# Routed blocks written out with constant waits, three engines' orders rearranged, a third up chunk in single-pass products

## What is computed

```python
def _ssm_forward(hidden_states, z, ...):            # z = layernorm(x)
    x = einsum('ed,bld->bel', in_proj_w, hidden_states)
    u = silu(conv4(x) + conv_b)
    dt_lo, Bm, Cm = split(einsum('ke,bel->bkl', x_proj_w, u))
    delta = softplus(einsum('er,brl->bel', dt_proj_w, dt_lo) + dt_proj_b)
    state = state * exp(d_t * A) + (d_t * u_t) * B_t          # scan over 512 steps, 16 states
    y = (state . C + D * u) * silu(z)

def _L0_ffn_ref(x, ...):                             # x = layernorm(x)
    aff = sigmoid(x @ wa); topk_p, topk_i = top_k(aff, 2); combine = normalised weights
    expert(x) = (gelu(x @ g + gb) * (x @ w1 + b1)) @ w2 + b2
    return x + sum of 2 shared experts + sum over 16 routed experts of combine * expert(x)
x = x + ssm;  x = x + ffn(layernorm(x))
```

## Time and profile before

| | us |
|---|---|
| median of 3 runs | 877.4 (876.62 to 882.0) |
| the profiled execution | 879.89 |
| its span | 877.7 |
| TensorE busy in the span | 784.8 |
| VectorE, ScalarE, GpSimd busy | 669.4, 524.3, 553.9 |

### The profile page before, as it was taken

The page is one execution under the profiler, slowest core; times in us unless marked ns, Lnnn a source line. Parts: engine busy times, 40 slices in busy tenths (PEclk is TensorE's granted clock), DMA queues, the critical chain, the costliest instruction groups (busy, mean ns, idle before and its releaser), DMA issues.

```text
span 877.7 us, 16086 instructions
## 1 busy us (share of the span) xinstructions
PE 784.8 (89%) x4384; PEld 587.4 (67%) x4385; DVE 669.4 (76%) x860; ACT 524.3 (60%) x884; POOL 553.9 (63%) x348
## 2 busy tenths in 40 slices
PE   6963799999999988998899999999999999999992
PEld 3622688888888877887777878886555555555550
DVE  4999999999999998999596759545656656565561
ACT  3896899999999999995332532023444333443330
POOL 9551399989999999999815560221434744454432
PEclk9975799999999999999999999999999999999996
DMA  6010311111141113201220121255558877876663
GB/s 183 1 55 0 106 52 62 56 54 51 59 157 49 49 49 109 60 14 49 97 96 1 49 90 55 96 228 238 115 142 242 215 208 186 186 196 177 159 139 48
DMA packets 35384, 91.65 MB, mean 104 GB/s; under 512 B 8716, under 2 KB 9228, under 8 KB 32000
## 3 DMA queue, kind: packets, MB, share of 16 engines
q1 hardware_dynamic: 23360, 65.50, 21.8%
q0 software_dynamic: 11968, 25.44, 14.3%
HBM read 122.24 MB, written 21.36 MB: 164 GB/s over the span
## 4 chain that ended last, share of the span: by engine, by line
PE 41%; DVE 17%; SPq 14%; issue 9%; POOL 8%; ACT 6%; DMA 3%; DVEq 0%; ACTq 0%; POOLq 0%
DVE r L1051 12%; PE ps L1451 6%; PE ps L1554 5%; PE ps L1453 5%; PE ps L1452 5%; POOL r L527 5%; PE ps L1577 5%; SPq L390 4%; SPq L391 3%; SPq L392 3%; PE ps L1790 3%; PE ps L1555 3%; SPq L393 3%; PE ps L1809 2%; POOL split L532 2%
## 5 line engine op out<-in xcount | busy, mean ns | idle before, releaser
L527 POOL TENSOR_TENSOR r<-r,mem 128x1024 f32<-128x1024 f32 x127 | 297.8, 2378 | 34.7 <-DVE r L1051 34.1
L1051 DVE TENSOR_TENSOR_SCAN r<-r,ps 128x1024 f32<-128x1024 f32 x128 | 286.8, 2277 | 9.7 <-issue 9.0
L752 ACT ACTIVATE r<-mem,nega 128x511 f32<-128x511 f32 x256 | 167.0, 715 | 1.8 <-DVE r L1051 1.7
L1554 PE MATMUL ps<-ident,mem 128*128 128x128 f32 x768 | 130.4, 279 | 28.4 <-DVE r L1051 21.7
L1577 PE MATMUL ps<-ident,r 128*128 128x128 f32 x1024 | 132.5, 273 | 3.7 <-DVE r L1081 2.4
L767 ACT ACTIVATE mem<-mem,b_turned 128x512 f32<-128x512 f32 x192 | 124.8, 715 | 8.6 <-PE ps L1555 8.0
L1554 PEld LDWEIGHTS ps<-ident,mem 128*128 128x128 f32 x768 | 87.4, 142 | 53.8 <-issue 52.8
L1577 PEld LDWEIGHTS ps<-ident,r 128*128 128x128 f32 x1024 | 115.8, 141 | 4.3 <-DVE r L1081 2.6
L1555 PE MATMUL ps<-mem 128*128 128x128 f32 x512 | 99.7, 277 | 0.0
L917 ACT COPY mem<-ps 128x256 f32<-128x256 f32 x47 | 17.5, 373 | 128.4 <-PE ps L1798 125.8
L1451 PE MATMUL ps<-split 128*128 128x512 f32 x216 | 87.3, 404 | 4.3 <-issue 1.7
(11 more groups left out here) (209 smaller groups left out, 1263.7 us busy)
## 6 DMA issues: line engine op xcount, KB each, us to landing
r<-in_r_up SPq DMA_DIRECT2D x47, 1024.0 KB
mem<-in_r_down SPq DMA_DIRECT2D x47, 512.0 KB
mem<-cm_rows SPq DMA_DIRECT2D x64, 256.0 KB, 3.2
mem<-in_r_b SPq DMA_DIRECT2D x4, 2048.0 KB, 12.3
out<-acc POOLq DMA_DIRECT2D x17, 256.0 KB, 2.9
r<-in_x SPq DMA_DIRECT2D x4, 1024.0 KB, 4.9
xn_scratch<-r SPq DMA_DIRECT2D x16, 256.0 KB, 2.7
mem<-in_ctx_t SPq DMA_DIRECT2D x4, 512.0 KB, 7.3
```

What stands on the lines that cost most here:

```text
L527: pool.tensor_tensor(state[:, k % 2, ec:ec + 2], state[:, k % 2, ec:ec + 2], c, ALU.mult).then_inc(s["weighed"], 1)
L752: act.activation(decay[:, k % 2, ec, 1:L], delta[:, b, ec, 1:L], ACT.Exp, scale=nega[:, ec, n:n + 1]).then_inc(s["decay_ready"], 1)
L1051: dve.tensor_tensor_scan(state[:, half, ec:ec + 2].rearrange("p e l -> p (e l)"), decay[:, half, ec:ec + 2].rearrange("p e l -> p (e l)"), ...
L1554: pe.transpose(ps[:, ec, lt * P:(lt + 1) * P], dbu_t[:, k % 2, lt, ec * P:(ec + 1) * P], ident[:])
```

## The change

- KSPLIT goes from 2 to 3: three of the four chunks of the up weights are split and go in single passes, one stays in full precision. `up_head`, `up_rest` and the token heads and rests grow by half; they lie over the first 12 tiles of `acc` rather than 8, so ScalarE's first head waits for 12 stored tiles. `blk_val_again` grows with it, and `half_i` moves into `row_i` to make room.
- The loops of TensorE, ScalarE and VectorE over routed blocks are written out; their waits have constant counts. VectorE keeps the register with the expert of a block from `hidden_bias` to `add_bias` instead of reading it again. SP's code is not changed.
- ScalarE's step was `weight_head(j+2)`, `turn_tokens(j+2)`, `hidden_gate(j)`, `turn_hidden(j)`; it is `turn_tokens(j+2)`, `hidden_gate(j)`, `turn_hidden(j-1)`, `weight_head(j+2)`. VectorE's `token_rest` is for j+2 instead of j+1.
- GpSimd: `rstd_first(1)` comes before the last `weight_rests`. In the routed stage the wait for `y_ready` comes after the waits for landings.
- ScalarE and VectorE treat the first two tiles of batch 1 ahead of the hidden values of shared product 2.

```diff
-KSPLIT = 2
+KSPLIT = 3
...
-            for c in range(2, 6):
+            for c in range(2, 5):
                 weight_rests(c)
             rstd_first(1)
+            weight_rests(5)
             base(0)
...
             gelu(3)
+            turn_normed(1, range(2))
             hidden_heads(2)
-            turn_normed(1)
+            turn_normed(1, range(2, LT))
...
-                act.copy(xgt[:, half], ps[:, 4 + half, KSPLIT * P:D]).then_inc(s["xgt_copied"], 1)
+                act.copy(xgt[:, half, 0:D - KSPLIT * P], ps[:, 4 + half, KSPLIT * P:D]).then_inc(s["xgt_copied"], 1)
...
             def step(j, round_, r):
-                if not isinstance(j, int) or j + 2 < NBLK:
-                    weight_head(j + 2, (r + 2) % RING, round_ + (r + 2) // RING)
+                if j + 2 < NBLK:
                     turn_tokens(j + 2, r % 2)
                 hidden_gate(j, r % 2)
-                turn_hidden(j, r % 2)
+                if j >= 1:
+                    turn_hidden(j - 1, (r - 1) % 2)
+                if j + 2 < NBLK:
+                    weight_head(j + 2, (r + 2) % RING, round_ + (r + 2) // RING)
...
-            act.wait_ge(s["early_stored"], 16 * NT // 2)
+            act.wait_ge(s["early_stored"], 16 * (NT - LT))
...
-            with act.Fori(1, (NBLK - 2) // RING) as jj:
-                for r in range(RING):
-                    step(RING * jj + r, jj, r)
+            for j in range(RING, (NBLK - 2) // RING * RING):
+                step(j, j // RING, j % RING)
...
             hidden_shared(3)
+            token_rests(1, range(2))
             hidden_rests(2)
-            token_rests(1)
+            token_rests(1, range(2, LT))
...
             def hidden_bias(j, half):
-                e = expert_of(j)
+                e = experts[j] = expert_of(j)
...
             def step(j, round_, r):
-                if isinstance(j, int) and j == 1:
-                    token_rest(2, 0)
                 hidden_bias(j, r % 2)
-                if not isinstance(j, int) or 1 < j < NBLK - 1:
-                    token_rest(j + 1, (r + 1) % 2)
+                if j + 2 < NBLK:
+                    token_rest(j + 2, r % 2)
                 hidden(j, r % 2)
-                if not isinstance(j, int) or j >= 4:
+                if j >= 4:
                     add_bias(j - 2, (r - 2) % RING, round_ + (r - 2) // RING)
...
-            with dve.Fori(2, (NBLK - 2) // RING) as jj:
...
-            with pe.Fori(1, (NBLK - 2) // RING) as jj:
```

More of the change, by code:

```diff
@@ L811, in gates, with turn_normed @@
                                    scale=rstd[:, ec:ec + 1]).then_inc(s["gate_ready"], 1)
-            def turn_normed(b):
-                for i, lt in enumerate(TILES[b]):
+            def turn_normed(b, places=range(LT)):
+                for i in places:
+                    lt = TILES[b][i]
                     act.wait_ge(s["xnt_ready"], b * LT + i + 1)
@@ L1119, in normed, with token_rests @@
                                       ALU.subtract, ALU.mult).then_inc(s["xn_ready"], 1)
-            def token_rests(b):
-                for i, lt in enumerate(TILES[b]):
+            def token_rests(b, places=range(LT)):
+                for i in places:
+                    lt = TILES[b][i]
                     dve.wait_ge(s["xnt_copied"], b * LT + i + 1)
@@ L1380, in token_rest @@
                                   ALU.subtract).then_inc(s["xgr_made"], 1)
+            experts = {}
             def hidden_bias(j, half):
-                e = expert_of(j)
+                e = experts[j] = expert_of(j)
                 dve.wait_ge(s["h_ready"], j + 1)
@@ L1392, in hidden @@
                 dve.wait_ge(s["hb_ready"], j + 1)
-                dve.scalar_tensor_tensor(out=hy[:, half], in0=hg[:, half], scalar=row_w[:, ds(j, 1)], in1=hb[:, half, F:2 * F],
+                dve.scalar_tensor_tensor(out=hy[:, half], in0=hg[:, half], scalar=row_w[:, j:j + 1], in1=hb[:, half, F:2 * F],
                                          op0=ALU.mult, op1=ALU.mult).then_inc(s["hy_ready"], 1)
             def add_bias(j, r, round_):
-                e = expert_of(j)
-                if not isinstance(j, int) or j >= RING:
-                    wait_apart(dve, s["y_odd" if r % 2 else "y_even"], 16 * (RING // 2 * round_ + r // 2 - 1))
+                e = experts[j]
+                if j >= RING:
+                    dve.wait_ge(s["y_odd" if r % 2 else "y_even"], 16 * (RING // 2 * round_ + r // 2 - 1))
                 dve.wait_ge(s["o_ready"], j + 1)
-                dve.scalar_tensor_tensor(out=y_sb[r], in0=tile(b2_all, e), scalar=row_w[:, ds(j, 1)], in1=ps[:, 6 + r % 2],
+                dve.scalar_tensor_tensor(out=y_sb[r], in0=tile(b2_all, e), scalar=row_w[:, j:j + 1], in1=ps[:, 6 + r % 2],
                                          op0=ALU.mult, op1=ALU.add).then_inc(s["y_ready"], 1)
             def step(j, round_, r):
-                if isinstance(j, int) and j == 1:
-                    token_rest(2, 0)
                 hidden_bias(j, r % 2)
-                if not isinstance(j, int) or 1 < j < NBLK - 1:
-                    token_rest(j + 1, (r + 1) % 2)
+                if j + 2 < NBLK:
+                    token_rest(j + 2, r % 2)
                 hidden(j, r % 2)
-                if not isinstance(j, int) or j >= 4:
+                if j >= 4:
                     add_bias(j - 2, (r - 2) % RING, round_ + (r - 2) // RING)
-                if isinstance(j, int) and j == 3:
+                if j == 3:
                     dve.wait_ge(s["loaded_b2"], 16 * 2)
@@ L1432, in _ @@
                 step(j, j // RING, j % RING)
-            with dve.Fori(2, (NBLK - 2) // RING) as jj:
-                for r in range(RING):
-                    step(RING * jj + r, jj, r)
+            for j in range(2 * RING, (NBLK - 2) // RING * RING):
+                step(j, j // RING, j % RING)
             for j in range((NBLK - 2) // RING * RING, NBLK):
@@ L1804, in down @@
                 pe.wait_ge(s[f"down_{r}"], 16 * (round_ + 1))
-                if isinstance(j, int) and j == 0:
+                if j == 0:
                     pe.wait_ge(s["so_added"], NT)
@@ L1816, in step @@
                 turn_hidden(j, r)
-                if not isinstance(j, int) or j + 3 < NBLK:
+                if j + 3 < NBLK:
                     turn_tokens(j + 3, (r + 3) % RING, round_ + (r + 3) // RING)
-                if not isinstance(j, int) or j >= 1:
+                if j >= 1:
                     down(j - 1, (r - 1) % RING, round_ + (r - 1) // RING)
```

22 lines of the change are left out of this document (12 added, 10 removed).

## The result

The changed kernel takes 868.73 us, median of 4 runs (866.54 to 872.21), beside 879.19 for the kernel before in the same runs (876.62 to 882.00). The ratio is 0.9882, with a 95% interval of 0.9853 to 0.9911: 1.2% faster, 10.4 us. The forecast was 4.9 us of gain and 872.5. The profiled execution is the quickest of the four (866.54, span 864.8), that of before one of the slower (879.89, span 877.7), so the two traces differ by 12.9 us, 2.5 more than the ratio gives.

The account below looks back on a forecast made before the run. TensorE looked like the bound, but SP's weight-load queue was taken to pace the routed stage. Gains 1.2 + 0.6 + 3.1 - 0.3, plus 0.3 for SP's earlier start, make 4.9: from 877.4 to 872.5 us, range 863.5 to 878.

Parts of the forecast that it names:

- SP paces: Routed stage: SP's weight-load queue sets the pace from about block 20; gain 4.9 us, own range 869 to 876, chance 0.55.
- TensorE paces: Rival for the routed stage: SP's beat only reflects TensorE's and quickens with it; 860 to 868 us, chance 0.25.
- the shift: VectorE's operation before the routed stage: ends 1.3 us earlier, near 431.5, of which 1.2 was counted.
- TensorE's block: Routed stage: third chunk in single passes saves TensorE 0.17 us a block, 8 us over 47; longer splits stay hidden.
- What SP makes of it: Routed stage: SP at 5.80 us a block falls behind TensorE at 5.32 and sets the end; gain 3.1 us.
- allowed lag: Routed stage: how late SP's up load may go out after its slot is free before TensorE waits, 7.0 us.
- On TensorE the turn costs nothing to be seen: Routed loops written out: block 16 to 17, across the loop's turn, takes 5.49 us, so removing turns adds nothing.
- nothing on the path: VectorE in the routed stage: dropping one of three register reads a block, ahead of the bias add, gains nothing.
- 9.0 us of waits: Routed stage, blocks 6 to 46 of the kernel before: waiting within 228.63 us, SP's queue 52% of the chain.
- Orders: Routed stage, new order of ScalarE's and VectorE's steps: takes off small late waits, bounds nothing and the whole 9.0 us.
- Before the stage: Ahead of the routed stage: GpSimd's reciprocal root comes 2.4 us earlier, after three weight rests, of which 1.2 is gained.
- Tail, -0.3: Last scatters after the routed blocks: 0.3 us of the gain lost as the last blocks come closer together.

Follow-up runs that it names:

- e1: Changed kernel with SP's three register reads made once a block and kept for the down load, and SP's loop written out: 860.23 us.
- e6: Changed kernel with one register read more in each of SP's loads (the slot is read twice): 914.78 us.
- e12: Changed kernel with only SP's loop written out, all six register reads of a block kept: 860.33 us.
- e8: Kernel before with only the loops of TensorE, ScalarE and VectorE written out: 876.07 us, ratio 0.9964.
- e7: Changed kernel with ScalarE's step put back in the order of before: 874.09 us, ratio 0.9928.
- e4: Changed kernel with KSPLIT back at 2, two chunks in single passes: 870.49 us, ratio 0.9880.
- e10: Changed kernel with VectorE's token rest one block ahead again, as before: 870.60 us, ratio 0.9908.
- e3: Kernel before with only the early edits: GpSimd's reciprocal root ahead of the fourth weight rest, split copies and rests of batch 1: 877.38 us, ratio 0.9988.
- e2: Kernel before with SP's register reads made once a block and SP's loop written out: 876.99 us, ratio 0.9958.
- e11: Kernel before with TensorE's, ScalarE's, VectorE's and SP's loops written out and SP's reads made once a block: 870.79 us, ratio 0.9930.
- e9: Changed kernel with ScalarE's old order, SP's reads made once a block and SP's loop written out: 865.88 us, ratio 0.9864.
- e5: Changed kernel with KSPLIT back at 2, SP's reads made once a block and SP's loop written out: 865.17 us, ratio 0.9834.

## Why the prediction was right, and where not

*The whole.* 868.7 lies inside the range, but 0.3 below the 869 to 876 that the likeliest case had for itself, and the ratio makes it faster by over 1%, which had 0.28. That case, SP paces, was right in kind: e1, e6 and e12 show it. Its gain was sized at 4.9 us and was 10.4. The time itself, 3.8 us under the 872.5, flatters: 872.5 was counted from 877.4, and the kernel before now has 879.19. And the stated range reached down to 863.5 for the sake of the second case, TensorE paces, which didn't come. Of the signs named, SP without waits, blocks 10 to 20 at 5.3, the head's waits for landings (over 15 us; 20.1) and the shift came true; block 45's product ended 11 us before 849.2, not 5.

No single edit carries the 10.4 us. Alone, the loops give 3.2 (e8, on the kernel before) and ScalarE's order 5.4 (e7, taken out of the changed kernel); the third chunk, the token rest and the early edits are not resolved one by one (e4, e10, e3), and GpSimd's wait wasn't tried.

*TensorE's block, 5.49 - 0.17 = 5.32.* Right, 5.33 measured; and right that SP hides it (e4 against the changed kernel). The rest grew to 1.76 us (1.84 expected), the head to 1.48 (1.57).

*The mis-sized step: "What SP makes of it".* I set the end by "block 45's load at 831.80, as before", plus 14.3 to the end of its up product. The load went out at 825.70, and the product ended 12.5 after it, at 838.20. Three errors. SP's run began 2.6 us earlier, as the stage did (626.04 for 628.64), and I had let 0.3 of that through. Its beat was 5.70, not 5.80: 3.5 us over 35 blocks, on the same instructions. In the seven kernels that keep SP's loop and reads (before, changed, e3, e4, e7, e8, e10) it lies between 5.69 and 5.81, so I took one execution's rate for a constant; part of the quicker trace is luck. And the landing at block 43 took 6.0 us where I had set 7.56 from one row. The allowed lag, 7.0 by the same row, becomes 18.4 - (6.0 + 1.48 + 1.76 + 0.4) = 8.8, and waits begin at block 24, not 20.

*"On TensorE the turn costs nothing to be seen", "nothing on the path".* The first is right; what was wrong, and the second real failure, is that the loops were given no cost anywhere. I looked for the loop's cost at its turn, on TensorE. It lies in every block, ahead of ScalarE's head and VectorE's rest, as the "issue" of 15.1 and 10.3 us that my own rows carried. e8 gives it 3.2 us under SP's pace, e2 and e11 a beat of 5.66 to 5.49 without.

*"9.0 us of waits", put down to SP.* In before they were of two limits at nearly one height. Each taken away alone gives 3 to 4 us (e2, e8); both together bring TensorE to its bare beat (e11). In the traces they help each other: the beat falls by 0.05 (e2), 0.09 (e8) and 0.23 (both). The timed runs don't show that: by the ratios it is 0.42% and 0.36% alone and 0.70% (0.44 to 0.96) together, a plain sum. The chain of waits names the one that ends last and is silent on the other.

*Orders.* I gave them between nothing and 9.0, and took the shorter way from landing to product, 3.1. e7 prices ScalarE's order at 5.4 us in the changed kernel, but mostly by way of GpSimd's scatters (e9), which I had not looked at. With two chunks the orders do nothing for the beat of the traced executions: e11 and e5 both have 5.49. Their medians are 5.6 us apart; of the 3.1 between the two spans 1.3 lie before the end of block 46's product and 1.8 behind it, and what the rest of the 5.6 is no trace shows.

*Before the stage.* Right in size for the place, 1.8 forecast and 1.9 (e3) to 2.3 measured at block 0, and the detail held. The timelines of GpSimd and VectorE in the changed kernel:

```profile
427.70 1.01 POOL L518 TENSOR_TENSOR rstd<-var_eps,minus_half 128x4 f32<-128x4 f32 x1
428.67 2.39 POOL L533 TENSOR_TENSOR split<-mem,split 128x1024 fp32r<-128x1024 f32 x1
```

```profile
428.74 2.34 DVE L1010 SCALAR_TENSOR_TENSOR shift<-meanvar,rstd 128x4 f32<-128x4 f32 x1 [1.12 <-POOL rstd L518]
```

The shift ended at 431.08 (431.5 forecast, 432.72 before). It again took as long as the GpSimd operation beside it, 2.34 us beside 2.39, as the forecast had it.

*Tail, -0.3.* The sign was wrong: from block 46's up product to the end are 21.7 us, before 23.0. I had left out the edit that puts GpSimd's wait for `y_ready` behind its register read. In the changed kernel a late bias add and its scatter:

```profile
840.51 0.75 DVE L1412 SCALAR_TENSOR_TENSOR sb_sb<-mem,row_w,ps 128x512 f32<-128x512 f32 x1
```

```profile
841.53 1.55 POOL L635 DMA_INDIRECT out<-sb_sb,ids  x1 [3.35 <-DMA out<-sb_sb,ids]
```

The scatter follows the add by 0.3 us. In the kernel before, where the register is read after the wait, it was 1.4:

```profile
848.51 0.75 DVE L1402 SCALAR_TENSOR_TENSOR sb_sb<-mem,row_w,ps 128x512 f32<-128x512 f32 x1 [0.74 <-issue]
```

and the scatter at 850.62. All profiles with the new GpSimd code have 21.6 to 22.1 us from block 46's product to the end (changed, e1, e4 to e7, e9, e10, e12), those with the old 23.0 to 23.5 (before, e2, e3, e8, e11). That edit wasn't tried alone, so its price is not shown.

## What to carry to other kernels

A chain of waits shows the limit that ends last, not how far below it the next one lies: before a limit's whole waiting time is credited to a change, look for "issue" idle in front of the operations on the next-best path (here 3.7 us came from taking away a limit that held 52% of the chain). Price a register read by the whole step from one to the next in the trace, not by its load instruction, and write out the loop of a queue that must issue a conditional DMA every few microseconds: here the 4 lines of SP's loop were worth more (868.7 to 860.3 us) than the third single-pass chunk. A queue that runs a few per cent slower than the engine it feeds costs nothing until its slack is used up, and then all of the difference.

## What was not expected of the hardware

- A register read from SBUF in SP's queue costs 0.61 us, of which the load itself is 0.27 in the median (e6); about one in seven takes over 0.3, and these 0.66 in the mean.
- Relieving SP took most of the scatter of the times away too. The kernels that keep SP's loop and reads have runs 4.0 to 6.5 us apart (the changed kernel 5.7 over four runs), those with SP relieved 0.5 (e1) to 3.4 (e2). That it comes from the spread of SP's beat (5.69 to 5.81 in seven kernels, one execution each) is likely but not shown.
- A long wait costs TensorE more than the wait itself. From 640 to 840 of the changed kernel, where it idles 1.1 us at most, the granted clock is 1.00 throughout. After idling 4.1 to 6.3 us in six of e6's eight long blocks, and 3.7 us in e9's, TensorE worked for some microseconds at the lower of its two levels, 1.2 in place of 2.4 GHz.
